# Sampled groups summed by halves and in pairs, attention's maxima in halves, negations on ScalarE, the values' bias ahead of queries and keys

## The chip, the cores and the metric

The kernel runs on one core of a Trainium2 chip. A core has TensorE (PE) for matrix products, VectorE (DVE), ScalarE (ACT), GpSimd (POOL) and SyncE (SP, which only starts transfers here). Each engine works through its own list of instructions in order and waits on semaphores for the others. The metric is the time of one execution on the device in microseconds (us), lower is better. Two layers of a vision network are computed in one launch.

## The reference

The input x has 4 images of 32 x 32 tokens with 128 features. Cut to what matters:

```python
x = x + conv(ln(x))        # deformable sampling, 8 groups x 9 points x 4 corners, 32 channels
x = x + moe(ln(x))         # 8 experts, 128 -> 512 -> 128, top 1, with a capacity
x = x + attention(ln(x))   # 8 heads of 16, a window of 7 x 7 keys, bias by position
x = x + moe(ln(x))

# conv, for each token and group
v = x @ v_w + v_b
samp = sum over 4 corners of v[y, x, group] * corner weight
out[group] = sum over 9 points of samp * weight      # so 36 products for each channel
return out @ out_w + out_b

# attention
attn = softmax(q . k_window + bias)                  # needs the row's maximum
out = attn . v_window;  return out @ Wproj + bproj

# moe
logits = x @ gate_w + gate_b; probs = softmax(logits); idx = argmax(probs)
pos = running count of tokens of that expert; kept = pos < C
y = ffn[idx](x) * prob * kept
```

All data is float32.

## The kernel before, in words

The 4096 tokens are 32 tiles of 128. A loop slot handles several tiles at different stages: in slot `i`, tile `i` is sampled, tile `i - 1` goes through the first mixture of experts, tile `i - 2` gets its queries, keys and values, tile `i - 3` its attention, and tile `i - 4` the second mixture of experts. A *unit* is one mixture of experts on one tile, and has eight *steps*, one for each expert (`e` = 0 to 7). In a slot the second mixture's unit comes first (`beside_second` lists what stands beside its steps), then the first mixture's unit (`beside_first`). The two functions are the order of the work: every engine runs them, each adding its own instructions, so a `conv`, `attend` or `dense` call at some step puts that part at the same place into each engine's list. Nothing is reordered afterwards, apart from the loads of ACT's function tables, which the compiler adds. Slots 0 to 3 and the last two are written out, the others are loops; after slot 31 come five more units with the rest of attention.

PE has, in each step, four products into a hidden bank `Z` (L1460), four products out of it into `Y` (L1470), and the parts beside it. ACT applies relu to `Z` with the result in `hid` (L1257).

The eight sampling groups are done in two ways.

- Six groups are *gathered*. POOL starts 54 indirect transfers for each tile (nine for each group, L778), each bringing a patch of four corners x 32 channels per token into `got` (128 x 1152 for each group). POOL may overwrite a group of `got` once DVE has summed that group of the tile before. On DVE, `conv(q)` multiplies the group by its weights in `held` (L998, 1152 elements) and adds up 36 values for each of 32 channels with one strided reduce (L1003) into `summed`. These are at: `conv(0)` step 4 and `conv(1)` step 6 of the second unit; `conv(2)` in two halves around attention's `weights` in step 0 of the first unit; `conv(3)` step 1, `conv(4)` step 2, `conv(5)` step 4.
- Two groups are *dense*. DVE builds 18 maps `made` (128 x 1024 each, L909, k = 0 to 17, three buffers), PE adds the transposed maps of nine k into the banks `N` (L1367), ACT copies the sum to `turns` (L1189), and PE multiplies with the values (L1376, "look-up"). The first maps of tile `i + 1` are made from step 3 of the first unit on, so `conv(5)` stands in the middle of them.

Attention on tile `i - 3`: DVE spreads the queries (L1110), PE makes the scores, DVE adds the bias (L1122), takes the maxima of all eight heads-by-columns (L1128) and negates them (L1130); ACT exponentiates four of the eight blocks in step 7 and four in step 0, with expert 0's and 1's relu between (L1304); DVE normalises (L1133, L1135); PE transposes (L1522), multiplies with the values (L1532) and projects (L1539); DVE adds the result to `X` (L1140), and the routing of the second mixture starts. The values' bias is added by DVE (L1102) after ACT has written Q and K (L1291, L1294).

Routing (`route`): DVE adds the gate's bias (L1032), takes the maximum (L1034) and its negative (L1036), ACT makes the exponential with it (L1239), DVE finds the chosen expert (L1037 to L1042). ACT needs another function table for this exponential than for the square root of the normalisation (L1230, L1282), so it loads a table twice for each routing.

## Time and profile before

| | |
|---|---|
| median of 3 runs | 2565.28 us (2561.62 to 2565.37) |
| the profiled execution | 2566.76 us, its span 2564.6 us |
| PE busy | 2176.9 us (85%) |
| DVE busy | 2071.5 us (81%) |
| ACT busy | 1303.8 us (51%) |
| POOL busy | 1693.2 us (66%), and 491.7 us between its transfers |
| mean granted clock of PE | 0.927 |
| L1003, strided reduce | 192 times, 412.7 us |
| L998, weighing | 192 times, 258.5 us |
| PE waits for `made` | 140.9 us |

The times of one profiled execution are read as positions on one clock that starts with the span; the tile's parts recur every 72 to 76 us in the steady loop. "Granted clock" is the share of full speed that PE's clock got. A busy PE is not a PE at full speed: the same eight products take about twice as long when the clock is down.

### The profile page before, as it was taken

The page shows a single profiled execution, that of the slowest core. Times are in us where ns is not written, and L with a number is a line of the kernel's source. Part 1 is how long each engine was busy: PE and PEld are TensorE (multiplying, and loading weights), DVE is VectorE, ACT ScalarE, POOL GpSimd, SP SyncE. Part 2 cuts the span into 40 slices and gives each one's busy share as a digit, 9 for nine tenths or more (in the row PEclk, how much of TensorE's full clock was granted, in tenths as well). Part 3 has the DMA queues.
Part 4 walks back from the last instruction along what each step waited for, and adds up shares of the span by engine and source line. Part 5 has one row for each costly group of instructions (what it writes and reads, how often), then busy time and mean ns, then how long its engine had stood idle before and what let it go on. Part 6 is the DMA issues. An engine that isn't in the chain of part 4 may idle for free.

```text
span 2564.6 us, 55196 instructions
## 1 busy us (share of the span) xinstructions
PE 2176.9 (85%) x17088; PEld 2051.1 (80%) x17088; DVE 2071.5 (81%) x3905; ACT 1303.8 (51%) x3855; POOL 1693.2 (66%) x1797
## 2 busy tenths in 40 slices
PE   1668798888989888889898888988888889898787
PEld 1467688888888888888898888888888888888777
DVE  4588888888888888888888888888888888887522
ACT  1223355555555555555555555555555555555555
POOL 2677777777777777767777767767777777777000
PEclk6778799999999999999999999999999999999898
DMA  8422222222222222222222222222121111211000
GB/s 189 139 63 60 59 60 65 65 66 64 64 59 56 64 63 63 63 59 64 58 56 65 63 61 63 63 57 57 52 60 55 55 57 56 57 49 58 10 23 4
DMA packets 220186, 157.92 MB, mean 62 GB/s; under 512 B 149994, under 2 KB 187516, under 8 KB 220124
## 3 DMA queue, kind: packets, MB, share of 16 engines
q0 software_dynamic: 55296, 113.36, 15.3%
q1 hardware_dynamic: 163804, 43.50, 7.7%
q8 instruction: 35, 0.57, 0.1%
q10 hardware_dynamic: 1024, 0.26, 0.0%
q14 instruction: 27, 0.22, 0.0%
HBM read 138.67 MB, written 18.04 MB: 61 GB/s over the span
## 4 chain that ended last, share of the span: by engine, by line
PE 61%; DVE 16%; ACT 9%; issue 7%; DMA 3%; SPq 2%; ACTq 1%; DVEq 1%; POOL 0%; POOLq 0%
PE N L1367 15%; PE Z L1460 14%; PE Y L1470 13%; DVE made L909 5%; PE N L1376 4%; ACT prob L1304 3%; ACT hid L1257 3%; DVE got L998 3%; PE N L1539 2%; DMA xt_m<-cold_T 2%; PE N L1532 2%; PE N L1522 2%; ACT L1230 1%; PE N L1514 1%; SPq L662 1%
## 5 line engine op out<-in xcount | busy, mean ns | idle before, releaser
L778 POOL DMA_INDIRECT got<-patches,ranks x1728 | 1677.3, 971 | 637.4 <-issue 491.7
L1257 ACT ACTIVATE hid<-Z,b 128x128 f32<-128x128 f32 x2048 | 580.9, 368 | 307.6 <-PE Z L1460 306.0
L909 DVE TENSOR_TENSOR made<-held,tent 128x1024 f32<-128x1024 f32 x576 | 679.4, 1217 | 46.2 <-PE N L1367 32.3
L1367 PE MATMUL N<-ident,made 128*128 128x128 f32 x4608 | 593.2, 283 | 144.2 <-DVE made L909 140.9
L1367 PEld LDWEIGHTS N<-ident,made 128*128 128x128 f32 x4608 | 529.9, 146 | 179.2 <-DVE made L909 127.1
L1470 PE MATMUL Y<-w,hid 128*128 128x128 f32 x4096 | 577.1, 286 | 50.1 <-ACT hid L1257 50.1
L1460 PE MATMUL Z<-xt_m,w 128*128 128x128 f32 x4096 | 584.1, 291 | 32.4 <-DMA xt_m<-cold_T 32.4
L1460 PEld LDWEIGHTS Z<-xt_m,w 128*128 128x128 f32 x4096 | 543.9, 206 | 45.3 <-DMA xt_m<-cold_T 21.7
L1470 PEld LDWEIGHTS Y<-w,hid 128*128 128x128 f32 x4096 | 524.5, 200 | 65.1 <-ACT hid L1257 56.8
L1003 DVE TENSOR_REDUCE summed<-got 128x32 f32<-128x1152 f32 x192 | 412.7, 2149 | 5.6
L998 DVE TENSOR_TENSOR got<-got,held 128x1152 f32<-128x1152 f32 x192 | 258.5, 1346 | 4.5 <-DMA got<-patches,ranks 0.8
L1376 PE MATMUL N<-v_dense,turns 128*128 (+1 forms) x1024 | 121.4, 273 | 6.2 <-ACT turns L1189 5.9
L1376 PEld LDWEIGHTS N<-v_dense,turns 128*128 128x128 f32 x1024 | 120.3, 193 | 8.0 <-ACT turns L1189 8.0
L1304 ACT ACTIVATE prob<-prob,soft 128x100 f32<-128x100 f32 x256 | 93.4, 371 | 54.8 <-DVE soft L1130 54.0
L1189 ACT ACTIVATE turns<-N 128x512 f32<-128x512 f32 x128 | 69.5, 595 | 67.7 <-PE N L1367 66.1
L1522 PE MATMUL N<-ident,prob 128*100 128x128 f32 x256 | 52.6, 374 | 44.9 <-DVE prob L1135 44.9
L1270 ACT ACTIVATE acc<-Y,small 128x128 f32<-128x128 f32 x64 | 23.4, 366 | 123.1 <-PE Y L1470 123.1
L1230 ACT ACT_TABLE_LOAD x63 | 80.8, 1283 | 1.8 <-ACT cold_T L1246 0.7
L1522 PEld LDWEIGHTS N<-ident,prob 128*100 128x100 f32 x256 | 40.7, 175 | 50.9 <-DVE prob L1135 50.3
L1239 ACT ACT_TABLE_LOAD x63 | 80.8, 1283 | 1.1
L1235 ACT ACTIVATE xt_m<-CV 128x1024 f32<-128x1024 f32 x32 | 32.8, 1025 | 95.5 <-PE CV L1439 95.5
L1196 ACT ACTIVATE summed<-N 128x32 f32<-128x32 f32 x64 | 12.6, 197 | 121.8 <-PE N L1376 121.8
(204 smaller groups left out, 2239.9 us busy)
## 6 DMA issues: line engine op xcount, KB each, us to landing
got<-patches,ranks POOLq DMA_INDIRECT x1728
vwin<-vpad SPq DMA_DIRECT2D x320, 40.0 KB
patches<-arena SPq DMA_DIRECT2D x92, 96.0 KB
w<-in_L_ffn_w SPq DMA_DIRECT2D x2, 2048.0 KB
patches<-got SPq DMA_DIRECT2D x38, 96.0 KB, 3.0
vpad<-vt SPq DMA_DIRECT2D x128, 16.0 KB
out<-X SPq DMA_DIRECT2D x32, 64.0 KB
xt_m<-cold_T ACTq DMA_DIRECT2D x64, 4.0 KB
```

What stands on the lines that cost most here:

```text
L778: pool.indirect_dma_start(out=got[:, q, j * PATCH:(j + 1) * PATCH], out_offset=None, in_=table, in_offset=bass.IndirectOffsetOnAxis(ap=ran ...
L909: v.tensor_tensor(made[:, k % MADE, :].rearrange("p (y x) -> p y x", y=H), across.unsqueeze(2).to_broadcast([P, H, W]), tent[:, 0, k, :].u ...
L998: v.tensor_tensor(g3, g3, wj.unsqueeze(2).to_broadcast([P, QJ * CORNERS, C]), ALU.mult)\
L1003: v.tensor_reduce(summed[:, q * C:(q + 1) * C], got[:, q, :].rearrange("p (j c) -> p c j", c=C), AX.X, ALU.add)\
L1230: a.activation(sd_m[:, 1:2], mv_m[:, 1:2], ACT.Sqrt, bias=eps[:, 0:1]).then_inc(*s("std"))
L1257: ins = a.activation(hid[:, e % 2, c, :], Z[e % 2][:, c * P:(c + 1) * P], ACT.Relu, bias=b1[n][:, e * FC + c:e * FC + c + 1])
L1304: ins = a.activation(prob[:, j, :], prob[:, j, :], ACT.Exp, bias=soft[:, 1, j:j + 1], accum_out=soft[:, 2, j:j + 1])
L1367: ins = pe.matmul(N[c // 4][:, (c % 4) * P:(c % 4 + 1) * P], made[:, k % MADE, c * P:(c + 1) * P], ident[:, :], start=(k % K == 0 and c % ...
L1376: ins = pe.matmul(N[0][:, 0:C], spread[:, c, :], v_dense[:, bass.ds(t // TB * TB + c, 1), n * C:(n + 1) * C] .rearrange("p o c -> p (o c)" ...
L1460: ins = pe.matmul(Z[e % 2][:, c * P:(c + 1) * P], w1[n][:, e, c * P:(c + 1) * P], xt_m[n][:, e, :], start=True, stop=True)
L1470: ins = pe.matmul(Y[:, 0:D], hid[:, e % 2, c, :], w2[n][:, e * FC + c, :], start=False, stop=(e == E - 1 and c == FC - 1))
L1522: ins = pe.transpose(N[j // 4][0:KK, (j % 4) * P:(j % 4 + 1) * P], prob[:, j, :], ident[:, :])
```

## The change

1. The groups are summed as the sets (0), (1), (2, 3), (4, 5). For each set DVE multiplies by the weights in one instruction, adds the second half of the 36 slabs to the first (`half`), the second quarter to the first (`fourth`), and reduces the nine that are left.
2. The set (2, 3) stands in step 1 of the first unit, the set (4, 5) in step 4. Steps 0 and 2 lose theirs. POOL waits for the set that a group belongs to.
3. Attention's maxima are taken in two halves, each right after its scores.
4. The negation of attention's maxima goes to ACT, in two halves ahead of the four exponentials each; so does the one in the routing.
5. DVE adds the values' bias as soon as PE's product is there; ACT's Q and K come after it.

```diff
-        conv_v = Steps(sem("conv_v"), "hold " + " ".join(f"m{q} r{q}" for q in range(NQ)) + " add")
+        conv_v = Steps(sem("conv_v"), "hold " + " ".join(f"m{q} half{q} fourth{q} r{q}" for q, *_ in SETS) + " add")
...
                     if e == 0:
                         if e1:
                             close(u1, 1, i - 4)
-                        conv(2, i, "weigh")
                         if att:
                             attend("weights", i - 3)
-                        conv(2, i, "reduce")
...
                             values("values", i + LEAD)
-                        conv(3, i)
+                        conv(2, i)
                     if e == 2:
...
-                        conv(4, i)
...
                         if not final:
-                            conv(5, i)
+                            conv(4, i)
...
-                            pool.wait_ge(*conv_v.done(f"r{q}", t - 1))
+                            pool.wait_ge(*conv_v.done(f"r{OF[q]}", t - 1))
...
-                    v.tensor_tensor(g3, g3, wj.unsqueeze(2).to_broadcast([P, QJ * CORNERS, C]), ALU.mult)\
+                    for k in group:
+                        v.wait_ge(*got_q[k].through(t))
+                    v.tensor_tensor(g4, g4, wj.unsqueeze(2).to_broadcast([P, n * SLABS, C]), ALU.mult)\
                         .then_inc(*s(f"m{q}"))
...
-                    v.tensor_reduce(summed[:, q * C:(q + 1) * C],
-                                    got[:, q, :].rearrange("p (j c) -> p c j", c=C), AX.X, ALU.add)\
+                    v.tensor_tensor(gs[:, :, 0:half], gs[:, :, 0:half], gs[:, :, half:2 * half], ALU.add)\
+                        .then_inc(*s(f"half{q}"))
+                    v.wait_ge(*d(f"half{q}", t))
+                    v.tensor_tensor(gs[:, :, 0:fourth], gs[:, :, 0:fourth], gs[:, :, fourth:2 * fourth], ALU.add)\
+                        .then_inc(*s(f"fourth{q}"))
+                    v.wait_ge(*d(f"fourth{q}", t))
+                    v.tensor_reduce(summed[:, q * C:(q + len(group)) * C].rearrange("p (n c) -> p n c", c=C),
+                                    gs[:, :, 0:fourth].rearrange("p n (s c) -> p n c s", c=C), AX.X, ALU.add)\
                         .then_inc(*s(f"r{q}"))
...
-                    v.wait_ge(*qkv_s.done("k", t))
+                    v.wait_ge(*qkv_t.done("qkv", t))
...
-                    v.wait_ge(*d("s1", t))
-                    v.tensor_reduce(soft[:, 0, :], prob, AX.X, ALU.max).then_inc(*s("max"))
-                    v.wait_ge(*d("max", t))
-                    v.tensor_scalar(soft[:, 1, :], soft[:, 0, :], -1.0, None, ALU.mult).then_inc(*s("neg"))
+                        v.wait_ge(*d(f"s{k}", t))
+                        v.tensor_reduce(soft[:, 0, 4 * k:4 * k + 4], prob[:, 4 * k:4 * k + 4, :], AX.X, ALU.max)\
+                            .then_inc(*s(f"max{k}"))
...
-                    a.wait_ge(*route_v[n].done("neg", t))
+                    a.wait_ge(*route_v[n].done("max", t))
+                    a.activation(small[n][:, 1:2], small[n][:, 0:1], ACT.Copy, scale=-1.0).then_inc(*s("neg"))
+                    a.wait_ge(*s_done("neg", t))
+                    a.wait_ge(*route_v[n].done("lg", t))
...
-                    a.wait_ge(*qkv_t.done("qkv", t))
+                    a.wait_ge(*qkv_v.done("v", t))
...
-                    a.wait_ge(*att_v.done("neg", t))
+                    a.wait_ge(*att_v.done(f"max{half}", t))
+                    a.activation(soft[:, 1, 4 * half:4 * half + 4], soft[:, 0, 4 * half:4 * half + 4], ACT.Copy,
+                                 scale=-1.0).then_inc(*s(f"neg{half}"))
+                    a.wait_ge(*att_s.done(f"neg{half}", t))
```

Three places of the order, each before and after. A row is line, operation, what it writes and reads, and the semaphores it waits for. Line numbers are those of the kernel that the row is from.

DVE in steps 0 to 2 of the first unit, from attention's normalisation to its residual add, before:

```order
L1135 TENSOR_TENSOR prob<-prob,soft 128x800 [waits att_v]
L1003 TENSOR_REDUCE summed<-got 128x32 [waits conv_v]
L888 TENSOR_TENSOR tent<-iota,spot 128x1152 [waits dense_v]
L799 TENSOR_TENSOR arena<-CV,vb 128x192 [waits values_out,val_t]
L801 TENSOR_TENSOR v_dense<-CV,vb 128x64
L998 TENSOR_TENSOR got<-got,held 128x1152 [waits got_3]
L1003 TENSOR_REDUCE summed<-got 128x32 [waits conv_v]
L998 TENSOR_TENSOR got<-got,held 128x1152 [waits got_4]
L1003 TENSOR_REDUCE summed<-got 128x32 [waits conv_v]
L1140 TENSOR_TENSOR X<-N,X 128x128 [waits att_t]
```

and after:

```order
L1143 TENSOR_TENSOR prob<-prob,soft 128x800 [waits att_v]
L888 TENSOR_TENSOR tent<-iota,spot 128x1152 [waits dense_v]
L799 TENSOR_TENSOR arena<-CV,vb 128x192 [waits values_out,val_t]
L801 TENSOR_TENSOR v_dense<-CV,vb 128x64
L1000 TENSOR_TENSOR got<-got,held 128x2304 [waits got_3,got_2]
L1007 TENSOR_TENSOR got<-got 128x2x576 [waits conv_v]
L1010 TENSOR_TENSOR got<-got 128x2x288 [waits conv_v]
L1013 TENSOR_REDUCE summed<-got 128x64 [waits conv_v]
L1148 TENSOR_TENSOR X<-N,X 128x128 [waits att_t]
```

The third to fifth group's six instructions around and behind `prob` become four for a pair, behind the values; nothing stands between the pair and the residual add.

DVE in steps 3 to 5, from the first `made` of the next tile on (`xn_m` is the normalised input of the second mixture's routing), before:

```order
L909 TENSOR_TENSOR made<-held,tent 128x1024 [waits dense_v,dense_t]
L909 TENSOR_TENSOR made<-held,tent 128x1024 [waits dense_t]
L1025 RECIPROCAL rs_m<-sd_m 128x1 [waits route1_s]
L1027 TENSOR_SCALAR xn_m<-X,mv_m,rs_m 128x128 [waits route1_v]
L909 TENSOR_TENSOR made<-held,tent 128x1024 [waits dense_t]
L998 TENSOR_TENSOR got<-got,held 128x1152 [waits got_5]
L1003 TENSOR_REDUCE summed<-got 128x32 [waits conv_v]
L909 TENSOR_TENSOR made<-held,tent 128x1024 [waits dense_t] x2
```

and after:

```order
L909 TENSOR_TENSOR made<-held,tent 128x1024 [waits dense_v,dense_t]
L909 TENSOR_TENSOR made<-held,tent 128x1024 [waits dense_t]
L1035 RECIPROCAL rs_m<-sd_m 128x1 [waits route1_s]
L1037 TENSOR_SCALAR xn_m<-X,mv_m,rs_m 128x128 [waits route1_v]
L909 TENSOR_TENSOR made<-held,tent 128x1024 [waits dense_t]
L1000 TENSOR_TENSOR got<-got,held 128x2304 [waits got_5,got_4]
L1007 TENSOR_TENSOR got<-got 128x2x576 [waits conv_v]
L1010 TENSOR_TENSOR got<-got 128x2x288 [waits conv_v]
L1013 TENSOR_REDUCE summed<-got 128x64 [waits conv_v]
L909 TENSOR_TENSOR made<-held,tent 128x1024 [waits dense_t] x2
```

Four instructions on twice the elements stand ahead of the fourth and fifth `made` (the row with x2), where there were two.

ACT in steps 5 to 7 of the first unit (`route, small` is the routing's exponential, `hid` expert relus, `hot_T` and `cold_T` the chosen experts' masks), before:

```order
L1257 ACTIVATE hid<-Z,b_0 128x128 [waits exp_t]
L1257 ACTIVATE hid<-Z,b_0 128x128 x3
L1239 ACT_TABLE_LOAD
L1239 ACTIVATE route,small<-route,small 128x8 [waits route1_v]
L1257 ACTIVATE hid<-Z,b_0 128x128 [waits exp_t]
L1257 ACTIVATE hid<-Z,b_0 128x128 x3
L1243 ACTIVATE hot_T<-M 8x128 [waits route1_t]
L1246 ACTIVATE cold_T<-M 8x128 [waits masked1]
```

and after:

```order
L1268 ACTIVATE hid<-Z,b_0 128x128 [waits exp_t]
L1268 ACTIVATE hid<-Z,b_0 128x128 x3
L1247 ACTIVATE small<-small 128x1 [waits route1_v]
L1250 ACT_TABLE_LOAD [waits route1_v]
L1250 ACTIVATE route,small<-route,small 128x8 [waits route1_s]
L1268 ACTIVATE hid<-Z,b_0 128x128 [waits exp_t]
L1268 ACTIVATE hid<-Z,b_0 128x128 x3
L1254 ACTIVATE hot_T<-M 8x128 [waits route1_t]
L1257 ACTIVATE cold_T<-M 8x128 [waits masked1]
```

The table load stood behind a relu and waited for nothing; it now stands behind the negation and waits for DVE (`route1_v`). In the second unit's routing the order changes in the same way.

## Rows read from the trace of the kernel before

**Rows 1.** Four tiles: stretch, length; busy PE, PEld, DVE, ACT, POOL; clock, DMA share, GB/s.

```profile
117.33:169.42 52.09, 30.20 (x194) 25.33 (x194) 50.66 (x70) 10.29 (x19) 35.81 (x38) 0.77 0.20 53
1190.60:1262.73 72.13, 64.87 (x536) 61.59 (x534) 64.31 (x119) 40.12 (x122) 53.10 (x56) 0.98 0.24 62
1407.81:1483.29 75.48, 67.22 (x535) 64.03 (x533) 64.31 (x120) 40.19 (x122) 54.73 (x59) 0.93 0.23 62
1483.29:1556.77 73.48, 64.83 (x537) 61.79 (x536) 64.23 (x119) 40.06 (x122) 52.01 (x54) 0.98 0.22 59
```

**Rows 2.** Timeline, DVE, the weights' copy of the fifth and 31st tile.

```profile
373.25 0.39 DVE L991 TENSOR_SCALAR held<-wq 128x216 f32 x1
...
2295.32 0.38 DVE L991 TENSOR_SCALAR held<-wq 128x216 f32<-128x216 f32 x1
```

**Rows 3.** Timeline, PE: start, duration, line, tiles, [idle before, releaser].

```profile
1207.43 1.16 PE L1470 MATMUL Y<-w,hid 128*128 128x128 f32 x8 [1.48 <-ACT hid L1257]
...
1210.13 1.08 PE L1522 MATMUL N<-ident,prob 128*100 128x128 f32 x8 [1.55 <-DVE prob L1135]
...
1217.46 2.05 PE L1539 MATMUL N<-wp,PT 128*128 128x128 f32 x16
...
1223.94 3.03 PE L1367 MATMUL N<-ident,made 128*128 128x128 f32 x16 [2.16 <-DVE made L909]
...
1231.48 1.09 PE L1367 MATMUL N<-ident,made 128*128 128x128 f32 x8 [0.87 <-DVE made L909]
```

**Rows 4.** Timeline, DVE, same tile: stretch with the sixth group.

```profile
1220.73 0.27 DVE L1140 TENSOR_TENSOR X<-N,X 128x128 f32 x1
...
1226.74 1.34 DVE L998 TENSOR_TENSOR got<-got,held 128x1152 f32<-128x1152 f32 x1
...
1230.20 2.36 DVE L909 TENSOR_TENSOR made<-held,tent 128x1024 f32<-128x1024 f32 x2
```

**Rows 5.** Groups by line and shape, DVE: busy us, mean ns; ACT's last.

```profile
L1003 DVE TENSOR_REDUCE summed<-got 128x32 f32<-128x1152 f32 x192 | 412.7, 2149 | 5.6
...
L998 DVE TENSOR_TENSOR got<-got,held 128x1152 f32<-128x1152 f32 x192 | 258.5, 1346 | 4.5 <-DMA got<-patches,ranks 0.8
...
L1128 DVE TENSOR_REDUCE soft<-prob 128x8 f32<-128x800 f32 x32 | 31.6, 986 | 1.1
...
L1196 ACT ACTIVATE summed<-N 128x32 f32<-128x32 f32 x64 | 12.6, 197 | 121.8 <-PE N L1376 121.8
```

**Rows 6.** Waits in total: us, times, longest.

```profile
DVE vt L1102 <- ACT KT L1294: 54.6, 32, 4.1
```

**Rows 7.** Timeline, ACT, the exponentials' start.

```profile
1202.12 1.14 ACT L1257 ACTIVATE hid<-Z,b 128x128 f32<-128x128 f32 x4 [0.41 <-PE Z L1460]
...
1204.81 0.38 ACT L1304 ACTIVATE prob<-prob,soft 128x100 f32<-128x100 f32 x1 [1.56 <-DVE soft L1130]
```

**Rows 8.** Timeline, ACT, table loads and what follows the second.

```profile
1229.94 1.28 ACT L1239 ACT_TABLE_LOAD   x1
...
1233.05 0.30 ACT L1239 ACTIVATE route<-route,small 128x8 f32<-128x8 f32 x1 [1.82 <-DVE small L1036]
...
1260.89 1.28 ACT L1239 ACT_TABLE_LOAD   x1
...
1262.18 0.30 ACT L1239 ACTIVATE route<-route,small 128x8 f32<-128x8 f32 x1
...
1263.68 1.08 ACT L1189 ACTIVATE turns<-N 128x512 f32<-128x512 f32 x2 [0.17 <-PE N L1367]
```

**Rows 9.** Timeline, PE, the dense groups' second look-up.

```profile
1265.27 1.87 PE L1376 MATMUL N<-v_dense,turns 128*128 x16
```

**Rows 10.** The same view, a short stretch in the fourth of those tiles.

```profile
1525.10:1528.40 3.30, 3.30 (x18) 3.30 (x17) 3.09 (x11) 1.53 (x6) 2.56 (x3) 0.52 0.20 60
```

**Rows 11.** Timeline, PE, third tile of rows 1: after the exponentials.

```profile
1427.36 1.95 PE L1522 MATMUL N<-ident,prob 128*100 128x128 f32 x8 [1.55 <-DVE prob L1135]
```

**Rows 12.** Timeline, POOL, first gather of a tile.

```profile
1267.58 1.83 POOL L778 DMA_INDIRECT got<-patches,ranks  x1 [2.29 <-DVE summed L1003]
```

More of the change, by code:

```diff
@@ L79 @@
 MADE = 3
+SETS = [(0,), (1,), (2, 3), (4, 5)]
+OF = {q: group[0] for group in SETS for q in group}
+SLABS = K * CORNERS
 PLACES = ("norm", "turn", "offsets", "places", "corners")
@@ L307, in build @@
         qkv_t = Steps(sem("qkv_t"), "xT qkv")
[L308 to L309 removed]
+        att_v = Steps(sem("att_v"), "qbd s0 max0 s1 max1 rsum norm add")
+        att_s = Steps(sem("att_s"), "neg0 exp0 neg1 exp1 p0 p1 o0 o1")
         att_t = Steps(sem("att_t"), "s0 s1 p0 p1 o proj")
@@ L985, in conv @@
                 if isinstance(part, int) and placed != "reduce":
-                    q = part
+                    q, group = part, next(group for group in SETS if group[0] == part)
                     if q == 0:
@@ L994, in conv @@
                         v.wait_ge(*d("hold", t))
-                    g3 = got[:, q, :].rearrange("p (j c) -> p j c", c=C)
-                    wj = held[:, weights_at + q * QJ * CORNERS:weights_at + (q + 1) * QJ * CORNERS]
-                    v.wait_ge(*got_q[q].through(t))
-                    v.tensor_tensor(g3, g3, wj.unsqueeze(2).to_broadcast([P, QJ * CORNERS, C]), ALU.mult)\
+                    n = len(group)
+                    g4 = got[:, q:q + n, :].rearrange("p n (s c) -> p (n s) c", c=C)
+                    wj = held[:, weights_at + q * SLABS:weights_at + (q + n) * SLABS]
+                    for k in group:
+                        v.wait_ge(*got_q[k].through(t))
+                    v.tensor_tensor(g4, g4, wj.unsqueeze(2).to_broadcast([P, n * SLABS, C]), ALU.mult)\
                         .then_inc(*s(f"m{q}"))
                 if isinstance(part, int) and placed != "weigh":
-                    q = part
+                    q, group = part, next(group for group in SETS if group[0] == part)
+                    gs = got[:, q:q + len(group), :]
+                    half, fourth = SLABS // 2 * C, SLABS // 4 * C
                     v.wait_ge(*d(f"m{q}", t))
-                    v.tensor_reduce(summed[:, q * C:(q + 1) * C],
-                                    got[:, q, :].rearrange("p (j c) -> p c j", c=C), AX.X, ALU.add)\
+                    v.tensor_tensor(gs[:, :, 0:half], gs[:, :, 0:half], gs[:, :, half:2 * half], ALU.add)\
[6 more added lines that the diff above has]
+                                    gs[:, :, 0:fourth].rearrange("p n (s c) -> p n c s", c=C), AX.X, ALU.add)\
                         .then_inc(*s(f"r{q}"))
```

15 lines of the change are left out of this document (6 added, 9 removed).

## The prediction

> **What bounds the kernel now.** I read the per-tile stretches first, then each engine's timeline through one tile, then the shapes. The steady loop handles one tile of 128 tokens in 72.13 to 75.48 us [rows 1]; the weights' copy at L991 stands once in each, and its starts in the fifth and the 31st tile give (2295.32 - 373.25) / 26 = 73.93 us on the mean [rows 2]. PE is busy for 65 to 67 us of that, DVE for 64, so neither has more than 8 to 10 us to spare, and the order inside the tile decides. In the tile at 1190.60 (period 72.13) PE waits at four places: 1.48 and 1.55 us around attention's exponentials, 2.16 us for the first `made`, 0.87 us for the fourth (k = 3) [rows 3]. The first two are a chain DVE maxima, ACT exponentials, DVE norm; the last two are DVE being late. From about 1240 on PE hardly waits until it comes back to the exponentials.
>
> The third part is PE's clock. The tile at 1190.60 has 0.98 of full clock, that at 1483.29 as well but 73.48 us, that at 1407.81 has 0.93 and 75.48 us [rows 1]. After the waits at the exponentials the eight transposes took 1.08 us in one tile and 1.95 us in another [rows 3, 11]: 2.4 against 1.2 GHz, set by whether the clock fell after those waits. After the wait for k = 3 in the tile at 1483.29 it stood at 0.52 for 3.3 us of busy PE [rows 10]; that tile is 73.48 - 72.13 = 1.35 us longer than the one where it fell only after the 2.16 us wait, whose cost DVE's lateness swallows (16 transposes took 3.03 us against 1.09 for eight, and 0.87 us of waiting was still left) [rows 1, 3].
>
> POOL isn't a bound: its first gather of a tile has waited 2.29 us, the last part of it for DVE's sum [rows 12].
>
> **DVE's stretch from `add` to `made` 3.** Starting at 1220.73 with attention's add and ending at 1230.20 + 1.2 = 1231.4, it holds the sixth group's weighing and sum (1226.74 to 1230.20, 3.46 us) [rows 4]. Now it holds the fifth and sixth. A tensor_tensor costs 1346 ns at 1152 elements, so about 1.04 ns each and 150 ns fixed; the contiguous reduce (986 ns at 800) has the same rate, the strided one (2149 ns at 1152) 1.735 ns each [rows 5]. Weigh 2304: 2.55; first halves 1152: 1.35; second 576: 0.75; reduce 576, strided like before: 0.15 + 1.00 = 1.15; the steps wait for each other, 0.02 more in all: 5.82 us, which is 2.36 more. The bounds for the unmeasured reduce: 0.75 us if it ran at the contiguous rate, 2.35 us if the old loss of 0.8 us was 25 ns for each of its 32 sums and now comes for 64. I take the stride: the 800-element reduce shows nothing per sum.
>
> The stretch starts earlier, for two reasons. PE's projection ends at 1217.46 + 2.05 = 1219.51 [rows 3], while the add starts at 1220.73 behind the fifth group's sum; with that moved it starts 0.2 after PE, 1.03 earlier. The other 1.0 comes from the exponentials, below. Sum: 2.36 - 2.03 = +0.3 us for `made` 3. The pair in step 2 (5.8 us) ends before PE's projection, by about 1.7 us: three groups were there and in step 0 before, now two. It costs nothing; without that cover its 5.8 us would be PE's wait.
>
> **Exponentials.** `v` no longer waits for ACT's K (54.6 us in 32 times, about 1.7 each [rows 6]; 1.1 us is gained, as PE's product now bounds it), and group 2's shorter sums give 3.46 - 3.22 = 0.24. Half maxima on DVE then are ready before ACT is free: ACT's previous work ends at 1202.12 + 1.14 = 1203.26, the first exponential started at 1204.81 [rows 7]. With a small ACT copy for the negation (197 ns for 128x32 [rows 5], taken as 0.22 with its wait) it starts at 1203.5, 1.3 earlier. The second negation takes 0.25 back: 1.0 us gained at PE's transposes. PE's wait of 1.48 shrinks to 0.15, that of 1.55 grows to 1.8, since the second negation lies in it. Q and K start 0.2 later behind `v`; PE has expert products until it needs K.
>
> **The table load.** This speaks against the change. ACT's exponential in the routing needs a table load of 1.28 us. Before, the load stood ahead of the wait: loaded at 1229.94, idle 1.82, exponential at 1233.05; loaded at 1260.89, exponential at 1262.18 [rows 8]. The order shows the load now behind the negation, and the negation waits for DVE's maximum. In the second unit the maximum is there at 1261.8; negation 0.2, load 1.28: the exponential starts 1.2 later. ACT's copies at 1263.68 had waited 0.17 for PE, so they end 1.0 later, 1265.77; PE's look-up started at 1265.27 [rows 8, 9] and now at 1265.8: +0.55 us, nothing covers it. In the first unit load and exponential end 1.7 later than at 1233.05; this lies beside the slower PE of the next part and I count 0 (up to 0.95 if the clock stays up). Bounds for both: 0 and 1.5.
>
> In this trace the exponential starts 0.01 us after the load's end [rows 8]. The Trainium skill ("ScalarE: Activation LUTs", section "What ACT_TABLE_LOAD costs") puts a drain of some 1.4 us behind each load. By that page, as an estimate, the look-up would come 0.55 + 1.4 us late; the row says otherwise and decides.
>
> **PE's clock.** PE reaches `made` 3 about 1.0 us (exponentials) plus 1.0 (no long wait for `made` 0) plus 1.0 (no half speed there) earlier than at 1230.6, and `made` 3 comes 0.3 later: the 0.87 us wait becomes about 4.5 us. It is longer than any wait after which the clock fell, so it falls in each tile, at a cost of 1.35 us as in the tile at 1483.29; 0.65 if half the slow time passes inside the wait, 2.2 if it lasts longer. At the exponentials one wait of 1.8 stands in place of 1.48 + 1.55. Before, this place fell in some tiles and not in others; I take half, at 1.7 us (3.4 us at half speed on PE's own path): 0.85.
>
> The Trainium skill ("TensorE: Matmul & The Clock Gate", section "Why this matters for your kernels") warns of long gaps between bursts of matmuls. By that rule, taken for long single gaps alone, only the new wait would count, which is the mild case below; the trace disagrees with it so far, as the clock fell after 1.5 + 1.55 us [rows 11].
>
> **Sum.** A tile: 72.13 + 0.30 + 0.55 + 1.35 + 0.85 = 75.2 us, 1.27 above 73.93; 27 tiles: +34. The first tiles are DVE's own (50.66 us busy of 52.09 [rows 1]), and it loses 2 x 0.24 + 2 x 1.1 = 2.7 us of work in each: 2.7 for the first, about 1 for each of the next three: -5.5. In the last tile the pair lies on the chain (+2.4), attention's steps of the last tiles save about 1 each: 0. Together +29 on the profiled 2566.76 (span 2564.6): 2596. That execution is 1.5 above the median 2565.28, so 2594.
>
> **Rivals.**
> - *Heavy:* the clock falls at the exponentials in every tile and stays low longer at `made` 3. 75.2 + 0.85 + 0.5 = 76.6: +72 - 5.5, 2632; with the first alone 2617. For it: 1.8 us in one piece. Against: the clock held through single waits of 1.5. Chance 0.17.
> - *Mild:* it never falls there. 74.35: +11 - 5.5, 2571. Chance 0.18.
> - *Faster:* the 4.5 us wait swallows the slow time (0.65 instead of 1.35), and there is no fall at the exponentials: 73.65, -7.5 - 5.5, 2552. It decides from the point where clock costs fall under 0.95 us a tile. For it: the slow time before was swallowed at 1223.94. Chance 0.13.
> - *The change doesn't save DVE time:* 25 ns per sum. +1.2 a tile: 2627. Chance 0.04.
> - *POOL becomes the bound:* the third group is released with the fourth. It is 23 us after the first, and POOL needs about 23 for the first two groups; with tiles longer than before it has time. Chance 0.01.
>
> The forecast has 0.47, with 2580 to 2610 of its own. The measurement can't tell less than 0.2% (5 us) from no change. Under 2560: 0.12; to 2570: 0.11; above: 0.77. Range 2558 to 2622, which takes in the mild case, the heavy one's lower part and the bounds of the reduce and the load.
>
> **What would show it.** The profile after should show: reduces of 64 sums near 1.15 us; the pair in step 5 at 5.8 us; PE's wait for `made` 3 at 4 to 5 us with the clock low after it, in every tile; the wait before attention's transposes at 1.8; the load behind the negation, and the second copies of `turns` 1 us later; DVE's busy time down by some 85 us (32 x 2.7). It is wrong if PE's wait before `made` 3 stays under 2 us, or if the load stands ahead of its wait.

## The result, and the profile after

The changed kernel takes 2614.22 us (median of 4 runs, 2608.32 to 2617.15) against 2563.45 us before (4 runs, 2558.2 to 2565.37): ratio 1.0206, 95% interval 1.0176 to 1.0236. The prediction was 2594 us with a range of 2558 to 2622 and 0.77 for slower. The profiled execution took 2608.32 us, its span is 2605.9, 41.3 above the span before.

The page of the changed kernel: each engine's busy time, share and instructions, and the instruction queue (packets, MB, share).

```profile
PE 2168.0 (83%) x17088; PEld 2038.5 (78%) x17088; DVE 1984.8 (76%) x3969; ACT 1320.7 (51%) x3983; POOL 1745.3 (67%) x1797
...
q14 instruction: 26, 0.21, 0.0%
```

DVE has 86.7 us less work than before (2071.5), and the kernel is slower all the same. The same stretches as in [rows 1]: the first tile, a steady one, and the 26 tiles from the fifth copy of the weights to the 31st.

```profile
122.09:171.90 49.81, 31.47 (x194) 26.60 (x194) 48.17 (x73) 9.16 (x17) 34.82 (x35) 0.76 0.21 53
1285.27:1360.22 74.95, 65.10 (x533) 61.82 (x532) 61.45 (x122) 40.66 (x125) 54.24 (x56) 0.95 0.22 58
384.19:2336.14 1951.95, 1704.52 (x13841) 1619.13 (x13840) 1596.97 (x3132) 1054.02 (x3211) 1443.43 (x1481) 0.95 0.22 59
```

The mean tile is 1951.95 / 26 = 75.07 us, against 73.93 [rows 2]. Tiles were uneven before, 72.1 to 75.8 us by the copies of the weights: in 11 of the 26 (74.8 to 75.8 us) PE's clock was at half for 6.8 us from the exponentials on and again after `made` 3, the others were 72.1 to 73.5. Now most are 75.0. PE's waits in total (us, times, longest):

```profile
PE N L1381 <- DVE made L909: 210.8, 67, 12.0
PE N L1536 <- DVE prob L1143: 52.1, 30, 1.8
...
PE N L1390 <- ACT turns L1197: 16.5, 24, 2.3
...
PE Y L1484 <- ACT hid L1268: 8.9, 17, 4.0
```

The last row answers to the wait of 1.48 us in [rows 3]; in the 26 steady tiles it is all but gone (1.1 us in all, where the kernel before has 40.1). In the tile at 1285.27, PE's timeline (start, duration, line, tiles, idle before and its releaser):

```profile
1288.48 1.97 PE L1390 MATMUL N<-v_dense,turns 128*128 x16 [0.48 <-ACT turns L1197]
...
1304.47 1.08 PE L1536 MATMUL N<-ident,prob 128*100 128x128 f32 x8 [1.79 <-DVE prob L1143]
...
1317.14 2.22 PE L1381 MATMUL N<-ident,made 128*128 128x128 f32 x16 [1.03 <-DVE made L909]
...
1327.09 1.97 PE L1381 MATMUL N<-ident,made 128*128 128x128 f32 x8 [4.78 <-DVE made L909]
```

PE waits 4.78 us for `made` 3, and its next eight products take 1.97 us instead of 1.09: the clock is down. DVE in the same place, with the pair:

```profile
1313.99 0.29 DVE L1148 TENSOR_TENSOR X<-N,X 128x128 f32 x1 [1.53 <-PE N L1553]
...
1320.03 2.54 DVE L1000 TENSOR_TENSOR got<-got,held 128x2304 f32<-128x2304 f32 x1
1322.61 1.36 DVE L1007 TENSOR_TENSOR got<-got 128x1152 f32<-128x1152 f32 x1
1324.00 0.76 DVE L1010 TENSOR_TENSOR got<-got 128x576 f32<-128x576 f32 x1
1324.79 1.12 DVE L1013 TENSOR_REDUCE summed<-got 128x64 f32<-128x576 f32 x1
1325.83 2.34 DVE L909 TENSOR_TENSOR made<-held,tent 128x1024 f32<-128x1024 f32 x2
```

The pair takes 1325.83 - 1320.03 = 5.80 us. ACT's timeline shows the second unit's table load behind the negation, the first half's negation of attention, and the first unit's load:

```profile
1284.45 0.20 ACT L1247 ACTIVATE small<-small 128x1 f32<-128x1 f32 x1 [0.98 <-DVE small L1044]
1284.75 1.28 ACT L1250 ACT_TABLE_LOAD   x1
1286.05 0.30 ACT L1250 ACTIVATE route<-route,small 128x8 f32<-128x8 f32 x1
...
1287.27 1.06 ACT L1197 ACTIVATE turns<-N 128x512 f32<-128x512 f32 x2
...
1298.65 0.22 ACT L1314 ACTIVATE soft<-soft 128x4 f32<-128x4 f32 x1
...
1328.48 0.21 ACT L1247 ACTIVATE small<-small 128x1 f32<-128x1 f32 x1 [6.85 <-DVE small L1044]
1328.78 1.28 ACT L1250 ACT_TABLE_LOAD   x1
```

The granted clock (third number from the right) during and after the wait for `made` 3, and around the exponentials, by stretches:

```profile
1324.10:1330.90 6.80, 3.81 (x18) 3.81 (x19) 6.59 (x12) 1.90 (x5) 5.28 (x6) 0.51 0.16 48
...
1303.60:1307.00 3.40, 2.53 (x21) 2.48 (x22) 2.95 (x5) 1.82 (x6) 2.79 (x3) 1.00 0.14 39
```

So in this tile the clock stays up through the wait of 1.79 us and is at half for 6.8 us around the other one. In the first tiles DVE waits for gathers (0.8 us in all before):

```profile
DVE got L1000 <- DMA got<-patches,ranks: 10.9, 3, 7.6
```

Where the 41.3 us of span are, by the copies of the weights: 4.8 ahead of the first tile (122.09 against 117.33), 6.2 in the first four tiles (262.10 against 255.92), 29.9 in the 26 tiles, 0.5 behind them.

### The profile page after: what moved, and what is told of

The parts are those of the page before. It is cut to its first block, busy times and chain, and to the rows that moved or that the text cites. A ratio compares the mean times of both kernels' runs of the same rounds, so it can differ in the third digit from the quotient of the medians.

```text
span 2605.9 us, 55608 instructions
## 1 busy us (share of the span) xinstructions
PE 2168.0 (83%) x17088; PEld 2038.5 (78%) x17088; DVE 1984.8 (76%) x3969; ACT 1320.7 (51%) x3983; POOL 1745.3 (67%) x1797
## 4 chain that ended last, share of the span: by engine, by line
PE 60%; DVE 14%; ACT 10%; issue 6%; POOL 3%; DMA 3%; SPq 2%; ACTq 1%; DVEq 0%; POOLq 0%
PE Z L1474 15%; PE N L1381 14%; PE Y L1484 12%; PE N L1390 4%; DVE made L909 4%; POOL got L778 3%; DVE got L1000 3%; ACT hid L1268 3%; ACT prob L1318 3%; PE N L1553 2%; DMA xt_m<-cold_T 2%; PE N L1528 2%; PE N L1546 2%; DVE got L1007 2%; SPq L662 2%
## 5 line engine op out<-in xcount | busy, mean ns | idle before, releaser
L778 POOL DMA_INDIRECT got<-patches,ranks x1728 | 1728.7, 1000 | 626.1 <-issue 504.2
L1381 PE MATMUL N<-ident,made 128*128 128x128 f32 x4608 | 603.8, 286 | 214.7 <-DVE made L909 210.8
L1484 PE MATMUL Y<-w,hid 128*128 128x128 f32 x4096 | 565.6, 282 | 9.8 <-ACT hid L1268 8.9
L1484 PEld LDWEIGHTS Y<-w,hid 128*128 128x128 f32 x4096 | 514.4, 197 | 24.4 <-ACT hid L1268 16.4
L1000 DVE TENSOR_TENSOR got<-got,held 128x2304 f32<-128x2304 f32 (+1 forms) x128 | 249.2, 1947 | 14.5 <-DMA got<-patches,ranks 10.9
L1007 DVE TENSOR_TENSOR got<-got 128x1152 f32<-128x1152 f32 (+1 forms) x128 | 135.6, 1060 | 4.4
L1247 ACT ACTIVATE small<-small 128x1 f32<-128x1 f32 x64 | 13.0, 204 | 227.9 <-DVE small L1044 227.9
L1013 DVE TENSOR_REDUCE summed<-got 128x64 f32<-128x576 f32 (+1 forms) x128 | 114.6, 896 | 4.4
L1536 PE MATMUL N<-ident,prob 128*100 128x128 f32 x256 | 39.5, 304 | 52.1 <-DVE prob L1143 52.1
L1010 DVE TENSOR_TENSOR got<-got 128x576 f32<-128x576 f32 (+1 forms) x128 | 77.9, 608 | 4.4
```

The lines of the kernel that those rows point to most:

```text
L778: pool.indirect_dma_start(out=got[:, q, j * PATCH:(j + 1) * PATCH], out_offset=None, in_=table, in_offset=bass.IndirectOffsetOnAxis(ap=ran ...
L1000: v.tensor_tensor(g4, g4, wj.unsqueeze(2).to_broadcast([P, n * SLABS, C]), ALU.mult)\
L1007: v.tensor_tensor(gs[:, :, 0:half], gs[:, :, 0:half], gs[:, :, half:2 * half], ALU.add)\
L1013: v.tensor_reduce(summed[:, q * C:(q + len(group)) * C].rearrange("p (n c) -> p n c", c=C), gs[:, :, 0:fourth].rearrange("p n (s c) -> p n ...
L1381: ins = pe.matmul(N[c // 4][:, (c % 4) * P:(c % 4 + 1) * P], made[:, k % MADE, c * P:(c + 1) * P], ident[:, :], start=(k % K == 0 and c % ...
L1484: ins = pe.matmul(Y[:, 0:D], hid[:, e % 2, c, :], w2[n][:, e * FC + c, :], start=False, stop=(e == E - 1 and c == FC - 1))
```

## The experiments

Twelve kernels in three groups of four, each group on one chip with the kernel before (2564.19, 2560.28 and 2553.51 us in the three), so ratios are compared, not times. The changed kernel's own ratio was measured beside another execution of the kernel before. Steps are numbered from 0, as in the kernel: the pairs stand in steps 1 and 4, which the prediction calls step 2 and step 5. An expectation's "fifth step" is step 4 too, and "the second" and "the fourth" in that of run 7 are steps 2 and 4.

**Run 1: the routing's negation back on DVE.**

```
-a.activation(small[n][:, 1:2], small[n][:, 0:1], ACT.Copy, scale=-1.0)     # ACT, route "logits"
+v.tensor_scalar(small[n][:, 1:2], small[n][:, 0:1], -1.0, None, ALU.mult)  # DVE, behind the maximum
```

> The changed kernel (2614 us) with one part undone: the routing's negation is on DVE again, so that ACT's table load stands ahead of its wait. If the load behind the negation costs 0.5 us a tile on PE's path in the second unit and nothing in the first, the tile goes from 75.1 to 74.5 us and the time to about 2600; PE's wait of 0.48 us before the second look-up (L1390) is gone. If the load costs in both units, about 1.5 us a tile: 2575. If it is hidden in both, 2614, as before this edit.

Measured: 2670.12 us, ratio 1.0417 (1.0358 to 1.0476). Nobody expected that. The tiles of the first loop are 76.6 to 80.2 us long, most of them 78.5, those behind it 73.4 to 75.8. DVE's waits, its timeline in one tile, and the instruction queue:

```profile
DVE made L909 <- issue: 88.1, 44, 4.1
```

```profile
1382.44 1.23 DVE L909 TENSOR_TENSOR made<-held,tent 128x1024 f32<-128x1024 f32 x1 [3.66 <-issue]
```

```profile
q14 instruction: 117, 0.96, 0.1%
```

The last row before that stall is the loop's branch on DVE's queue (duration three times over, first and last start in this stretch):

```profile
L489 DVEq COMPARE_BRANCH  x1: 63/63/63, 1378.7 to 1378.7; - x1
```

DVE stands 3.66 us behind the branch, waiting for nothing that the profile shows, and the queue moved 117 packets instead of 26. DVE's work is no longer (1988.5 us busy, 1984.8 in the changed kernel); the suspicion is that its instructions are fetched again in each turn. Run 5 tests that.

**Run 2: the pair in step 4 taken apart.** The fifth group alone in step 2, the sixth alone in step 4.

```
-SETS = [(0,), (1,), (2, 3), (4, 5)]
+SETS = [(0,), (1,), (2, 3), (4,), (5,)]
 if e == 2:  ... places("turn", ...)
+    conv(4, i)
 if e == 4:  ... if not final:
-    conv(4, i)
+    conv(5, i)
```

> The changed kernel with the fifth group alone in step 2 and the sixth alone in step 4, each still summed by halves (3.2 us each); third and fourth stay together. If the pair in DVE's stretch is what costs: the sixth takes 2.6 us less there, the residual add comes 1.6 us later behind the fifth, so made 3 comes 1.0 us earlier and PE's wait for it falls from 4.8 to about 2.2 us; the tile 73.8 us, the time about 2580. If the table load and the negations carry the loss and the placing doesn't matter: within 5 us of 2614.

Measured: 2549.53 us, ratio 0.995 (0.9922 to 0.9977), mean tile 72.96: a little faster than before, and 30 us faster than the 2580 that were expected if the pair is what costs. The fifth and sixth group as a pair in step 4 are the costly part, and the rest of the change is worth something.

**Run 3: PE kept busy in the wait.** 32 transposes of a constant between the third and fourth product with `made`.

```
-dense("sum", i + 1, range(2, 4))
+dense("sum", i + 1, range(2, 3))
+for _ in range(32): pe.transpose(CV[:, 0:P], ident[:, :], ident[:, :])
+dense("sum", i + 1, range(3, 4))
```

> The changed kernel with 32 transposes of the identity into an unused part of a PSUM bank, about 3.5 us of PE, in PE's list between made 2 and made 3, where PE waits 4.8 us. Nothing reads them. If the fall of the clock after this wait costs: made 3 comes at the same place, its eight transposes take 1.1 and not 2.0 us, and the tile becomes 1.5 to 1.9 us shorter: 2563 to 2573 us. If PE's clock isn't what makes the tile longer behind made 3 (table load and masks instead): within 5 us of 2614, or slower.

Measured: 2599.83 us, ratio 1.0151 (1.0089 to 1.0212), far from the 2563 to 2573 of the clock theory. The wait for `made` 3 fell to 1.32 us and the clock holds there, but in most tiles it now falls some 5.5 us behind the copy of the weights, near the look-up, where PE had waited 0.48 us. PE's timeline of such a tile; then the stretch of its fall, a tile without any, and that tile as a whole.

```profile
1213.92 1.97 PE L1401 MATMUL N<-v_dense,turns 128*128 x16 [0.48 <-ACT turns L1201]
...
1254.01 1.09 PE L1392 MATMUL N<-ident,made 128*128 128x128 f32 x8 [1.32 <-DVE made L913]
```

```profile
1216.20:1219.60 3.40, 3.40 (x17) 2.96 (x17) 2.05 (x9) 0.99 (x4) 2.58 (x3) 0.50 0.13 40
...
1436.17:1509.86 73.69, 67.29 (x569) 63.85 (x568) 61.55 (x121) 40.40 (x125) 53.57 (x55) 1.00 0.22 58
1210.71:1285.74 75.03, 68.28 (x565) 64.71 (x564) 61.67 (x121) 40.52 (x125) 54.01 (x57) 0.98 0.22 60
```

The tile without a fall is 73.69 us, so the clock costs 75.0 - 73.7 = 1.3 us a tile in the changed kernel, and 1.34 in the other place. Run 2 gives back 75.07 - 72.96 = 2.1 us a tile, so the clock isn't all of it.

**Run 4: the kernel before with sums by halves alone,** six single groups at their old places; negations, maxima and values as before.

```
 v.tensor_tensor(g4, g4, wj..., ALU.mult)                                        # as before
-v.tensor_reduce(summed[:, q * C:(q + 1) * C], got[:, q, :].rearrange("p (j c) -> p c j", c=C), AX.X, ALU.add)
+v.tensor_tensor(gs[:, :, 0:half], gs[:, :, 0:half], gs[:, :, half:2 * half], ALU.add)
+v.tensor_tensor(gs[:, :, 0:fourth], gs[:, :, 0:fourth], gs[:, :, fourth:2 * fourth], ALU.add)
+v.tensor_reduce(summed[...], gs[:, :, 0:fourth].rearrange("p n (s c) -> p n c s", c=C), AX.X, ALU.add)
```

> The kernel before with the sums by halves alone: six groups, each alone and where it was (3.22 instead of 3.46 us each); attention, routing and the values' bias as before. If the arithmetic of the shapes holds, DVE's stretch is 0.24 us shorter and its start 0.24 us or more earlier: 0.25 to 0.5 us a tile, 2550 to 2558 us beside 2563. If waits on the steps in between eat it: 2563.

Measured: 2565.56 us, ratio 1.0009 (0.9984 to 1.0033). DVE has 49 us less work (2022.4 against 2071.5) and the time doesn't change. In the profiled execution the mean tile is 73.64 us instead of 73.93, and 7.2 us are lost ahead of the fifth tile. The tiles are of two kinds: 15 of the 26 are 74.5 to 75.2 us long, the others 71.2 to 72.6. One of each kind, and the stretch at the exponentials of the long one:

```profile
1114.65:1189.64 74.99, 67.57 (x536) 64.38 (x534) 62.84 (x131) 40.27 (x122) 56.44 (x60) 0.93 0.23 62
1264.59:1336.56 71.97, 64.60 (x536) 61.18 (x534) 62.66 (x131) 40.25 (x122) 54.32 (x57) 0.98 0.23 63
1133.30:1140.00 6.70, 5.98 (x26) 5.77 (x27) 6.56 (x10) 2.93 (x9) 5.18 (x6) 0.50 0.29 64
```

The long tiles are at half clock for 6.8 us from the exponentials on and again after `made` 3, the short ones for 3.4 us or not at all.

**Run 5: run 1 with its loop moved by twelve instructions.**

```
+for _ in range(12):
+    v.sem_inc(passed, 1)      # ahead of the loop; nothing waits for it
```

> The changed kernel with the routing's negation back on DVE, as in the run at 2670.12 us, and twelve more semaphore instructions on DVE ahead of its first loop, which move that loop's instructions by twelve places and leave the loop as it was. Theory (the loop's instructions are fetched again in every turn where they lie badly in the blocks in which DVE's instructions are fetched): the 117 packets of the instruction queue fall to about 27, the 88.1 us that DVE waited for nothing shown ahead of made fall to about 11, the mean tile falls from 77.4 to about 74.5 us, and the time is 2590 to 2605 us, below the changed kernel's 2614 by what the table load behind the wait costs. Rival (the negation on DVE itself, with its place in the exponential's chain, makes the turn longer): 2660 to 2675 us with the same packets.

Measured: 2603.91 us, ratio 1.0178 (1.0156 to 1.02), as the theory had it. Packets and DVE's wait without a releaser:

```profile
q14 instruction: 27, 0.22, 0.0%
```

```profile
DVE made L909 <- issue: 11.0, 26, 0.5
```

So 2.4% of run 1 was instruction fetch, shown by moving the code alone. The Trainium skill ("Runtime: NRT & Kernel Launch", section "Instruction fetch mechanics") says that a taken branch whose target has left the window of fetched instructions stalls the engine; the 117 packets and the 3.66 us agree. Run 5 is now the changed kernel with its negation on DVE, and the changed kernel is 0.3% above it. Its tile shows what happens when something is saved beside the clock: PE's timeline at the exponentials, and two stretches of the clock.

```profile
1299.56 1.92 PE L1536 MATMUL N<-ident,prob 128*100 128x128 f32 x8 [1.79 <-DVE prob L1146]
```

```profile
1299.60:1303.00 3.40, 3.40 (x15) 3.19 (x16) 1.69 (x4) 1.19 (x2) 2.94 (x2) 0.50 0.14 39
1323.50:1326.80 3.30, 2.96 (x14) 2.96 (x15) 3.16 (x9) 0.39 (x2) 2.42 (x3) 0.50 0.18 57
```

The same wait of 1.79 us that left the clock up in the changed kernel is followed by half clock here, in every tile of the first loop (21 of the 26), and the low time after `made` 3 is half as long. The tiles are 75.1 us in the loop: the look-up's half microsecond was saved and spent again on the clock.

**Run 6: the kernel before with its routing's negation on ACT,** the reverse edit of run 1.

> The kernel before with one part of the change alone: the routing's negation is on ACT, so that the table load stands behind ACT's wait for the maximum. The prediction's term of 0.55 us a tile (look-up of the second unit late): 2564 + 15 = about 2579 us, and the PE wait for turns on L1376 grows from 5.9 us to some 16 to 20 us. Rival (the load lies in ACT's free time, and what the look-up waits is taken from a later wait): 2560 to 2568 us. Rival (both units pay, 0.95 us and more): 2590 us and above.

Measured: 2557.93 us, ratio 0.9993 (0.9975 to 1.0011). The prediction's +0.55 a tile isn't in the time. PE's waits in the 26 steady tiles, the kernel before first, then run 6:

```profile
PE Y L1470 <- ACT hid L1257: 40.1, 26, 1.7
```

```profile
PE Y L1472 <- ACT hid L1259: 22.9, 20, 1.6
PE N L1378 <- ACT turns L1188: 9.0, 19, 0.5
```

The look-up is late as predicted (9.0 us in 19 times), and the next wait, for `hid`, shrinks by 17.2 us. But the late piece isn't paid out of that wait: the transposes behind it come 20.0 to 20.9 us after the copy of the weights, where the kernel before had 19.5 to 19.9. A tile in which the clock falls once, beside the first products with `made`, shows the price, 73.55 us for the 72.13 of the like tile at 1190.60 [rows 1]:

```profile
1409.60:1483.15 73.55, 65.07 (x535) 61.74 (x534) 64.08 (x117) 40.16 (x123) 52.68 (x57) 0.98 0.23 61
```

The kernel before has three such tiles in a row, 72.1 to 72.3 us, and run 6 has several of 73.6. So the load costs 1.4 us in tiles of this kind, near the prediction's upper bound. What hides it in the mean is the clock: the kernel before has 11 tiles with 6.8 us at half clock at the exponentials, run 6 has none, and its tiles are 72.5 to 74.9 us.

**Run 7: run 2 with the negation on DVE.**

> The changed kernel with the fifth group alone in the second step, the sixth alone in the fourth (2549.5 us so far), and the routing's negation back on DVE. If the table load behind the wait costs 0.5 us a tile here too: 2535 us (2530 to 2542). If it is hidden once the pair is gone: 2546 to 2553 us. If the instructions' place brings back the fetches of the 2670 us run: over 2600 us.

Measured: 2524.64 us, ratio 0.986 (0.9836 to 0.9884). Against run 2 (0.995) the negation on ACT costs 0.9%, some 23 us. The transposes stand 18.4 us behind the copy of the weights here, and 19.2 to 20.8 in the first loop of run 2.

**Run 8: the kernel before with halved sums and the new order of attention and values,** no pairs, the routing's negation on DVE; that is run 4 with these edits:

```
-v.wait_ge(*qkv_s.done("k", t))       # DVE: values' bias behind ACT's copies
+v.wait_ge(*qkv_t.done("qkv", t))
-a.wait_ge(*qkv_t.done("qkv", t))     # ACT: copies of q and k
+a.wait_ge(*qkv_v.done("v", t))
 (and the maxima and negations of attention by halves, as in the change)
-pe.wait_ge(*qkv_v.done("v", after))   # PE, ahead of the routing's transpose: v was last, now k is
+pe.wait_ge(*qkv_s.done("k", after))   # (also part of the change)
```

> The kernel before with the sums by halves in six single groups at their old places (2565.6 us so far), and the changed kernel's order of attention and values added: v ahead of the copies of q and k, maxima and their negations by halves. The prediction's term of 0.85 us a tile for the fall of the clock at the exponentials: 2588 us, mean tile 74.5, and falls of the clock some 18 us behind the start of most tiles. Mild theory (no fall there, and the earlier copies save a little): 2555 to 2568 us. Its distance to the changed kernel with its negation on DVE is what the two pairs cost.

Measured: 2513.35 us, ratio 0.982 (0.9799 to 0.9841). The part is worth 1.9%, where the expectation by the prediction's term of +0.85 us a tile was 2588 us. PE's waits in the 26 steady tiles, run 4 first (two rows), then run 8:

```profile
PE N L1535 <- DVE prob L1148: 40.3, 26, 1.6
PE Y L1483 <- ACT hid L1270: 35.0, 26, 1.6
```

```profile
PE N L1382 <- DVE made L912: 88.6, 54, 4.0
PE N L1537 <- DVE prob L1147: 46.4, 26, 1.8
```

In run 8 the row for `hid` L1269 at `Y` L1485 is down to 0.5 us. The granted clock over these 26 tiles is 0.98, against 0.95 in run 4. It falls at the exponentials here too, in 22 of the 26 tiles, but is back after 3.4 us:

```profile
1165.88:1237.54 71.66, 64.86 (x536) 61.56 (x534) 62.42 (x131) 40.50 (x124) 54.02 (x57) 0.98 0.24 63
1184.40:1187.80 3.40, 3.40 (x15) 3.19 (x16) 3.33 (x7) 1.20 (x2) 2.79 (x3) 0.51 0.17 49
```

The tiles of run 8's first loop are, but for the first two of them, 71.6 to 71.8 us long, like the short ones of run 4 (71.86 on the mean). Run 4's 15 long ones are 3.1 us longer, 46 of the 53 us between the two kernels' 26 tiles: the gain is for the most part the long tiles that are gone. One wait of 1.79 us stands in place of two close together; that this is why is not shown, since run 6 still has both waits in half of its tiles and no long stretch either.

**Run 9: run 5 with `made` 3 ahead of the pair.**

```
 if e == 4:
-    dense("make", i + 1, range(2, 3))
+    dense("make", i + 1, range(2, 4))
     ... conv(4, i)
 if e == 5:
-    dense("make", i + 1, range(3, 5))
+    dense("make", i + 1, range(4, 5))
```

> The changed kernel with its negation on DVE and its loop moved by twelve (2603.9 us so far), and DVE's product for made 3 ahead of the pair in the fifth step instead of behind it; made 4 stays behind the pair. Theory (the pair costs what it makes made 3 late, and PE's clock falls in that wait): PE's wait of 4.8 us goes, a wait of about 1 us for made 4 comes, mean tile 74.9 - 2.5 = 72.4 us, time 2535 us (2520 to 2550). Rival (the same lateness shows up whole at made 4): 2590 to 2610 us. Rival (POOL's gathers behind the later sums are what costs): 2590 us and above, with POOL's waits for summed as long as they are now.

Measured: 2560.75 us, ratio 1.0031 (1.0019 to 1.0044), mean tile 73.26. It gives back 1.5% of the 3.2% that the pair costs, about half, and no more: 2560.75 us lies between the 2520 to 2550 of the theory and the 2590 of its rivals. The waits in the 26 tiles:

```profile
PE M L1461 <- DVE route L1054: 111.5, 26, 4.3
...
PE N L1381 <- DVE made L909: 27.0, 26, 1.1
```

The 4.77 us for `made` 3 became 4.3 us for the routing's one-hot, the next thing that stands behind the pair on DVE. I had named `made` 4 as what would be late next, and it is (1.1 us), but had overlooked the row that the router waits for.

**Run 10: run 8 with `made` 3 ahead of the sixth group,** the same edit.

> The kernel of 2513.4 us (sums by halves of six single groups at their old places, attention and values in the new order) with made 3 ahead of the sixth group in DVE's list. PE waits 2.2 us for made 3 in each of its tiles. Theory: 1.9 us of it go, 27 tiles, 2465 to 2490 us. Rival (the wait comes back at made 4, or as a longer wait for the cold half or at attention's exponentials): 2505 to 2520 us. Slower: if the sixth group's later sum delays the projection's transposes and POOL.

Measured: 2505.22 us, ratio 0.9807 (0.9791 to 0.9823), no difference from run 8 that can be told. The waits moved as in run 9:

```profile
PE M L1462 <- DVE route L1055: 50.7, 26, 3.0
PE N L1382 <- DVE made L912: 47.2, 40, 2.1
```

**Run 11: the kernel before with the new order of attention and values alone,** sums whole.

> The kernel before with the new order of attention and values alone, its sums over whole groups. With halved sums the same order took 2565.6 us to 2513.4. If the two parts add up: 2512 us (2505 to 2520). If the order's gain is bound to the free time on DVE that the halves make: 2525 to 2550 us. If the prediction's term for the clock at the exponentials holds: 2587 us.

Measured: 2501.43 us, ratio 0.9785 (0.9764 to 0.9806), with run 12 the best: the gain needs none of the freed DVE time. None of its 26 tiles has a long low stretch at the exponentials, and the transposes, the add and `made` 3 all come 1.1 us earlier than in the tile at 1190.60 (18.4, 29.0 and 38.5 us after the copy of the weights).

**Run 12: run 8 with the maxima whole again and their negation on DVE,** so that the values' bias ahead of the copies is left.

> The kernel of 2513.4 us with the maxima whole again and the negation on DVE, so that only the values' bias ahead of ACT's copies of q and k is left of the attention part. The prediction had 1.1 us of the earlier exponentials from the bias and little from the halves: then 2515 to 2530 us. If the halves of the maxima are what removes PE's wait of 1.5 us for the hidden layer: 2545 to 2565 us.

Measured: 2500.53 us, ratio 0.9788 (0.9772 to 0.9805). The order of the values' bias carries the whole gain; the halves of the maxima bring none, and cost 0.3% if anything (the two were measured beside the kernel before on different chips). PE's wait before the transposes goes back from 46.4 us to 40.3, the same row as in run 4, which is the second negation's 0.24 us in each tile.

**The change as a chain of ratios,** each step one part more:

| kernel | ratio | step | in us |
|---|---|---|---|
| before | 1 | | |
| + sums by halves (run 4) | 1.0009 | +0.1% | +2 |
| + values' bias first, maxima in halves (run 8) | 0.982 | -1.9% | -48 |
| + third and fourth group together (run 7) | 0.986 | +0.4% | +10 |
| + fifth and sixth together, later (run 5) | 1.0178 | +3.2% | +81 |
| + routing's negation on ACT (changed) | 1.0206 | +0.3% | +7 |

Steps of 0.4% and less are near what the intervals allow. The step of +3.2% joins two groups and also moves the fifth from step 2 to step 4. No run has the two as singles in step 4, so how much is due to the joining and how much to the place isn't shown; by their rows two singles would be 0.64 us longer there than the pair.

## Why the prediction was right, and which terms of it were not

Right in direction and within its range, by 20 us too low; its two largest mechanisms are there, but several terms are wrong and partly make up for each other.

- **The pair:** 5.80 us for 5.82, the reduce of 64 sums 1.12 to 1.17 for 1.15, DVE's saving 86.7 for 85. Right by its rows.
- **The wait for `made` 3:** 4.78 us for "about 4.5", with the clock low after it in the steady tiles. Right. Run 3 prices the clock at 1.3 us a tile; the prediction had 1.35.
- **The tile's sum:** 75.07 us for 75.2 on the mean, 74.95 in the tile at 1285.27. From the copy of the weights to `made` 3 it was 39.60 us in the tile at 1190.60 and is 1325.83 - 1285.27 = 40.56, so +0.96 where 0.30 + 0.55 + 0.85 = 1.70 stood (the look-up that the table load makes late comes 2.5 us behind the copy); from there to the next copy it was 32.53 and is 34.39, +1.86 where 1.35 stood.
- **The fall of the clock at the exponentials in half of the tiles, 0.85 us: the step that failed.** The clock falls there in 3 of the 26 tiles, and not in this one. What is left of the 1.70 without it is 0.85 for the measured 0.96, and it is there piece by piece: the transposes come 0.33 us earlier in the tile (19.20 for 19.53) where 1.0 - 0.55 was predicted, the add at 28.72 where 28.1 + 0.55 was. As a part on its own the new order is worth -48 us (run 8 against 4), and -55 alone (run 11). The prediction had seen the wait of 1.48 go, but let it end in a longer wait for `made` 3. That is true only together with the pair, which is how the sum came out. It had also no term for the 11 tiles of the kernel before whose clock stayed low for 6.8 us at the exponentials; none is left.
- **What the pair costs:** the prediction made it +2.36 - 2.03 on DVE and 1.35 for the clock, 1.7 us a tile. Measured apart it is 74.90 - 71.80 = 3.1 us (run 5 against 7). Of the 2.03 us of earlier start that the prediction set against it, run 7 has 0.6 without the pair (its add starts at 29.56 behind the fifth group's sum, 30.13 before), so that part would have been gain. Run 9 adds that it is not `made` 3 alone that the pair hurts, but also the routing that stands behind it.
- **The table load, 0.55 us:** the place is right (0.48 us in the tile above), the size too small. With the load behind its wait the transposes come 0.8 us later (19.20 in the changed kernel, 18.40 in run 5), and the like tile of run 6 is 0.8 us longer up to `made` 3 and 0.6 behind it, where 0.55 for the second unit and 0 for the first were counted. So the term for the first unit's load, put at 0, is the likely part of the 0.5 us by which the stretch behind `made` 3 is over its 1.35. The time doesn't answer by a constant, as the clock's falls move with it: nothing in the kernel before (run 6), 23 us in run 2 against 7, 7 us in the changed kernel. The exponential starts 0.02 us after the load's end, so no drain shows here either.
- **The first tiles, -5.5 us: wrong.** The first four tiles take 6.2 us more together: the first 2.3 us less, as the prediction had it (2.7), the other three 8.5 us more. DVE waits 10.9 us for gathers instead of 0.8. By run these four tiles take 253.6 us without pairs (run 8), 259.2 with the third and fourth together (run 7), 261.9 with both pairs (run 5): a pair releases its gathers only at its end, which fits, but no run shows that POOL is the bound there. The prediction gave that 0.01. Why run 8 has 7.3 us of such waits and yet short tiles was not followed up. The 4.8 us ahead of the first tile are a transfer of the weights that is early or late in runs of kernels with the same start (118.11 in run 5, 122.35 in run 8), and not the change.
- **The difference of 20 us:** 12.8 us of span, of which the first tiles and what lies ahead of them make 16.4 and the steady ones -3; and 7.4 because the profiled execution lies 5.9 below this kernel's median, while the prediction took off 1.5 for the other.
- **Rivals:** *faster* and *mild* did not come, since the sum held; what they said of the exponentials (no fall there) is what the trace shows. *Heavy* has one half right, the longer low stretch at `made` 3.

**What stays open:** why the clock stays low for 6.8 us at the exponentials in some kernels and for 3.4 in others; why the clock, after the same wait of 1.79 us, holds in the changed kernel and falls in run 5, and how the pair's 3.1 us divide between lateness and clock when the falls move, and between joining the two groups and their place.

## What to carry to other kernels

Price a part of a change by what it does alone and with its neighbours: here a gain of 2% and a cost of 3% share one tile, and the sum from one best tile hid both. Joining two pieces of work on an engine saves its fixed costs, but it also moves one of them, and everything behind it then waits (here `made` 3 and the routing); before merging, list each row that stands behind the merged piece and who waits for it, and try the parts singly. An engine's total is no measure of the time (49 us less DVE work, no change), while moving one small instruction ahead of two copies brought some 2%. Where the clock falls in some tiles and not in others, compare tiles with the same falls: a mean that doesn't move can be a cost of 1.4 us a tile hidden by falls that went away (run 6).

## What the runs showed of the hardware

- **A loop can be fetched again in every turn by its place alone.** Run 1 against run 5: twelve semaphore instructions ahead of the loop take the packets from 117 to 27 and the time from 1.0417 to 1.0178 of the kernel before. Packets of the instruction queue and a wait on `issue` of some 3.7 us once a turn are the signs.
- **The clock's losses move rather than go.** Filling the wait after which it fell brought a fall near a wait of 0.48 us (run 3), and taking half a microsecond out of the tile brought one at a wait of 1.79 us that had been harmless (run 5). In run 4 the tiles with 6.8 us at half clock at the exponentials and more after `made` 3 are 3.1 us longer than the others (74.95 and 71.86 us on the mean).
- **Halving by wide adds ahead of a strided reduce gives little:** by the means of their shapes, weighing and sum of 1152 elements take 1350 + 760 + 459 + 651 = 3220 ns, for 3495 with the whole reduce [rows 5], and 2304 elements 5801 ns. The pair saves 0.64 us over two singles, far less than it cost.
